# A gated cross-attention and ternary feed-forward block: new order of all five engines' lists, with the loads of x tiles 2 and 3 and of context 1 behind the gate weights

## The reference, cut to what matters

```python
# attention over the row's own layer norm: scores (512 x 512) are multiplied by it
qp = ctx @ Wq.T + bq ; kp = ctx @ Wk.T + bk
scores = (qp @ kp.T) * H**-0.5 * layernorm(x)
x = x + tanh(g_xattn) * softmax(where(mask, -inf, scores))
# feed-forward, activations quantised to 8 bits by row, weights to -1, 0, 1
def qlinear(x, w):
    ws = mean(abs(w)) + EPS ; wq = clip(round(w / ws), -1, 1)
    xs = max(abs(x), -1) / 127 + EPS ; xq = clip(round(x / xs), -128, 127)
    return (xq @ wq.T) * xs * ws
h = silu(qlinear(layernorm(x), w_gate)) * qlinear(layernorm(x), w_up)   # 2048 wide
x = x + tanh(g_ffn) * qlinear(h, w_down)
```

## Time and profile before

| what | value |
|---|---|
| median of 3 runs | 224.48 us |
| fastest, slowest run | 224.33, 224.86 us |
| span of the profiled execution, first to last instruction | 222.5 us |
| the profiled execution's own time | not given apart from its span |
| mean granted TensorE clock | 0.944 of full |
| PE, DVE, ACT, POOL busy | 199.3, 180.2, 124.5, 97.8 us |

### The profile page before, as it was taken

One profiled execution on the slowest core, in us unless ns is written; L12 is line 12 of the kernel. 1 busy time (PEld: TensorE's weight loads), 2 busy tenths in 40 slices (PEclk: granted clock), 3 DMA queues, 4 the chain that ended last, 5 costly groups with the idle time before them and its releaser, 6 DMA issues.

```text
span 222.5 us, 2846 instructions
## 1 busy us (share of the span) xinstructions
PE 199.3 (90%) x854; PEld 90.3 (41%) x854; DVE 180.2 (81%) x359; ACT 124.5 (56%) x165; POOL 97.8 (44%) x154
## 2 busy tenths in 40 slices
PE   8764008999999998999999999999999999999994
PEld 7221004344444344444444444444444444444441
...
GB/s 215 420 423 423 417 391 424 281 325 8 3 47 47 115 186 172 98 0 3 47 64 121 153 91 15 69 80 74 141 3 175 201 89 13 96 79 16 97 188 94
DMA packets 47360, 32.84 MB, mean 148 GB/s; under 512 B 40944, under 2 KB 41072, under 8 KB 45808
## 3 DMA queue, kind: packets, MB, share of 16 engines
...
q10 hardware_dynamic: 144, 0.13, 0.3%
...
## 4 chain that ended last, share of the span: by engine, by line
PE 71%; DMA 14%; ACT 5%; DVE 4%; issue 2%; SPq 2%; DVEq 0%
PE pU L947 23%; PE pG L934 23%; PE pD L965 20%; DMA stage_b<-in_L_ffn_w_up 8%; DMA stage_a<-in_L_ffn_w_down 4%; PE pA L909 3%; ACT down_w L689 2%; DMA stage_b<-stage_b 2%; ACT L736 1%; ACT hid L736 1%; DVE abs_part L1345 1%; SPq L351 1%; PE pA L898 1%; ACT stage_b L743 1%; DVE am L1320 1%
## 5 line engine op out<-in xcount | busy, mean ns | idle before, releaser
L736 ACT ACTIVATE hid<-pG,act_g 128x512 f32<-128x512 f32 x64 | 43.6, 688 | 54.6 <-PE pG L934 54.4
L934 PE MATMUL pG<-gate_w,xqT 128*128 128x512 f16 x256 | 64.7, 388 | 1.4 <-DVE xqT L1303 0.8
L947 PE MATMUL pU<-up_w,xqT 128*128 128x512 f16 x256 | 62.7, 379 | 0.0
L965 PE MATMUL pD<-down_w,stage_b 128*128 128x512 f16 x256 | 57.3, 379 | 0.6 <-DMA stage_b<-stage_b 0.6
L1311 DVE TENSOR_TENSOR hid<-pU,hid 128x512 f32<-128x512 f32 x64 | 43.6, 685 | 11.1 <-PE pU L947 9.2
L934 PEld LDWEIGHTS pG<-gate_w,xqT 128*128 128x128 f16 x256 | 25.1, 100 | 37.0 <-issue 8.0
L965 PEld LDWEIGHTS pD<-down_w,stage_b 128*128 128x128 f16 x256 | 24.9, 98 | 31.8 <-issue 2.3
L947 PEld LDWEIGHTS pU<-up_w,xqT 128*128 128x128 f16 x256 | 25.1, 98 | 31.3 <-issue 1.7
L743 ACT ACTIVATE stage_b<-hid,inv 128x1024 f16<-128x1024 f32 x15 | 16.9, 1139 | 7.8 <-DVE inv L1329 7.8
L560 POOL TENSOR_SCALAR out_scale<-den,act_e,down_k 128x1 f32<-128x1 f32 x16 | 5.9, 371 | 33.4 <-DVE den L1326 33.4
L909 PE MATMUL pA<-kT,qT 128*128 128x512 f32 x26 | 15.4, 678 | 4.9 <-ACT kT L709 4.9
...
## 6 DMA issues: line engine op xcount, KB each, us to landing
stage_a<-in_L_ffn_w_gate SPq DMA_DIRECT2D x4, 1024.0 KB, 11.2
stage_b<-in_L_ffn_w_up SPq DMA_DIRECT2D x4, 1024.0 KB, 19.2
stage_a<-in_L_ffn_w_down SPq DMA_DIRECT2D x4, 1024.0 KB, 9.0
stage_b<-in_x SPq DMA_DIRECT2D x2, 1024.0 KB, 5.3
...
```

The source lines that it names most:

```text
L736: act.activation(hid[:, t % NH, n * 512:(n + 1) * 512], pG[c % NG][:, :], ACT.Silu, scale=act_g[:, t:t + 1]).then_inc(silu_done, 1)
L934: ins = pe.matmul(pG[c % NG][:, :], xqT[:, t // TILES % 2, t % TILES, k, :], gate_w[:, n, k, :], start=k == 0, stop=k == KD - 1)
L947: ins = pe.matmul(pU[c % NU][:, :], xqT[:, t // TILES % 2, t % TILES, k, :], up_w[:, n, k, :], start=k == 0, stop=k == KD - 1)
L965: ins = pe.matmul(pD[t % ND][:, :], hidT[:, t % 2, k, :], down_w[:, k // KD, k % KD, :], start=k == 0, stop=k == KI - 1)
```

## The change

It renews the order of all five lists, and beside this:

- `chunk`: tiles 2 and 3 are interleaved by group as tiles 0 and 1 are.
- The q projection of batch 1 goes to `pG[1]`, k of batches 0 and 1 to `pG[0]`; score(3) goes to `pA`, not to `pD[1]`. Projections no longer wait for one another's copy but for the last user of their bank (`wait_pA`). The first two gate groups wait for k and q of batch 1 to be copied out of `pG`.
- `ABS_BY` becomes `ABS_PIECES`: all abs sums on ACT (gate's chunk 3 in two halves), but for one half chunk of up on DVE.
- `SIGN_BY`: gate's chunk 0 and down's chunk 2 are rounded by DVE (V), gate's others by POOL.
- POOL's rounds don't wait for the bound of the chunk before. The negative of a group's maximum is replaced by the negative of `rstd1`, computed in `rstd`. `rgate` is computed for a group at once.
- SP loads x tiles 2 and 3 and context 1 behind the four gate chunks, x tiles 4-7 before the up chunks, and down's chunks 1 to 3 behind transposes. Stores stand later.

```diff
 def chunk(t, n):
-    return 2 * n + t if t < 2 else NC * t + n
+    return 2 * NC * (t // 2) + 2 * n + t % 2 if t < TILES else NC * t + n
...
-        first_banks = [pA, *pU, pD[-1]][:TILES]
+        q_banks = [pA, pG[1], pA, pA]
+        k_banks = [pG[0], pG[0], pA, pA]
+        score_banks = [*pU, pA]
...
-        RESIDUAL_BY = "VPVVPPPPPPPVPPPP"
-        CENTRE_BY = "APAAAAAAAPVPVAVV"
-        QUANTISE_BY = "PPPPPPPPAAVAVPVV"
+        RESIDUAL_BY = 'VPPVPPPPPVPPPPVP'
+        CENTRE_BY = 'VPAAVAAAVPVAAPPV'
+        QUANTISE_BY = 'PPPPPPPAVPPAVPPA'
...
-        HQ_BY = ["PA", "AP", "AA", "AA", "PA", "PA", "AP", "AA",
-                 "PA", "PV", "PP", "AV", "PA", "AP", "VV", "PV"]
+        HQ_BY = ['PA', 'AP', 'VP', 'PA', 'PV', 'AA', 'AP', 'PA', 'PA', 'PV', 'PP', 'PV', 'VP', 'PA', 'VV', 'PA']
...
-        ABS_BY = ["AAAV", "AVAA", "AAAA"]
-        SIGN_BY = ["QXXX", "QQQX", "XXQQ"]
+        ABS_PIECES = [[(0, 0, 2048, 'A'), (1, 0, 2048, 'A'), (2, 0, 2048, 'A'), (3, 0, 1024, 'A'), (3, 1024, 2048, 'A')], [(0, 0, 2048, 'A'), (1, 0, 2048, 'A'), (2, 0, 2048, 'A'), (3, 0, 1024, 'V'), (3, 1024, 2048, 'A')], [(0, 0, 2048, 'A'), (1, 0, 2048, 'A'), (2, 0, 2048, 'A'), (3, 0, 2048, 'A')]]
+        SIGN_BY = ['VQQQ', 'QXQX', 'XQVQ']
...
             load_ctx(0)
-            sp.dma_start(masks_u8[:, :], masks).then_inc(mask_loaded, 16)
             load_x(0)
-            load_x(1)
-            load_ctx(1)
+            load_masks()
             load_w(0, 0)
             load_w(0, 1)
             load_w(0, 2)
             load_w(0, 3)
+            load_x(1)
+            load_ctx(1)
+            load_x(2)
             load_w(1, 0)
             load_w(1, 1)
             load_w(1, 2)
             load_w(1, 3)
+            load_ctx(3)
+            load_w(2, 0)
             load_ctx(2)
-            load_ctx(3)
-            load_x(2)
-            load_w(2, 0)
+            load_x(3)
+            transpose_x(4)
             load_w(2, 1)
+            transpose_x(5)
+            transpose_hidden(1, 1)
             load_w(2, 2)
             load_w(2, 3)
...
-                if m or n:
-
-                    wait_ternary(pool, *divmod(NC * m + n - 1, NC))
...
             def project_k(b):
-                pe.wait_ge(q_ready, b + 1)
-                pe.matmul(pA[:, :], wk_s[:, :], ctx_s[:, b % NQ, :], start=True, stop=True).then_inc(k_done, 1)
+                if b >= 2:
+                    wait_pA(pe, "k", b)
+                elif b == 1:
+                    pe.wait_ge(k_ready[0], 1)
+                pe.wait_ge(ctx_loaded[b], 16)
+                pe.matmul(k_banks[b][:, :], wk_s[:, :], ctx_s[:, b % NQ, :], start=True, stop=True).then_inc(k_done, 1)
...
+            def weight_round(m, n):
+                dve.wait_ge(winv_done, m + 1)
+                dve.tensor_scalar(chunk_of(m, n), stages[m][:, n, :], winv[:, m:m + 1], None, ALU.mult)\
+                   .then_inc(w_round_dve, 1)
```

More of the change, by code:

```diff
@@ L592, in _ @@
             quantise_x(0)
[L593 to L594 removed]
+            quantise_x(1)
+            rstd(1)
+            exp_bias(1)
+            weight_round(0, 1)
+            weight_round(0, 2)
+            valid_sums(1)
+            gate_scales(0)
+            residual1(2)
+            weight_round(0, 3)
+            std2(1)
+            weight_round(1, 0)
+            quantise_x(2)
+            quantise_x(3)
+            mask(2)
             up_scales(0)
[L596 removed]
@@ L1395, in _ @@
+            inverse_x(0)
+            stats1(3)
+            score(2)
+            score(3)
+            mask_and_max(2)
+            mask_and_max(3)
             weight_scale(0)
-            stats2(1)
-            weight_abs(1, 1)
+            weight_round(0, 0)
+            copy_xT(0)
             weight_bound(0, 0)
+            weight_bound(0, 1)
+            stats1(4)
+            stats1(5)
             gate_sums(1)
-            absmax_x(0)
-            weight_bound(0, 1)
-            absmax_x(1)
@@ new lines, in _ @@
+            stats2(8)
+            stats2(9)
+            centre(8)
+            product(6, 3)
+            absmax_x(8)
+            absmax_x(9)
+            inverse_std2(4)
+            inverse_x(4)
+            quantise_x(8)
+            product(7, 0)
+            absmax_hidden(5, 1)
+            inverse_hidden(5)
+            product(7, 1)
+            product(7, 2)
+            stats2(10)
+            centre(10)
+            product(7, 3)
+            product(8, 0)
+            residual2(3)
@@ L1503, in _ @@
+            absmax_hidden(6, 0)
+            stats2(11)
+            absmax_hidden(6, 1)
+            absmax_x(10)
+            absmax_x(11)
+            reciprocal_scale(4)
+            inverse_x(5)
+            inverse_std2(5)
+            residual2(4)
+            inverse_hidden(6)
             stats1(12)
-            product(4, 3)
-            mask_and_max(11)
-            product(5, 0)
-            absmax_hidden(4, 1)
             stats1(13)
-            inverse_hidden(4)
-            product(5, 1)
+            score(12)
@@ L1579, in _ @@
+            absmax_x(12)
+            stats2(13)
+            product(10, 3)
+            product(11, 0)
+            absmax_x(13)
+            inverse_x(6)
+            inverse_std2(6)
+            quantise_x(12)
+            residual1(14)
+            stats2(14)
+            inverse_hidden(9)
+            quantise_hidden(9, 1)
+            product(11, 1)
+            absmax_x(14)
+            product(11, 2)
             residual2(7)
-            quantise_hidden(9, 1)
-            product(10, 3)
+            product(11, 3)
```

1043 lines of the change are left out of this document (513 added, 530 removed).

## The result

The changed kernel takes 225.44 us (median of 13 runs, 224.08 to 226.65), the kernel before 224.33 in the same job (13 runs, 223.88 to 224.86): ratio 1.0052, 95% interval 1.0033 to 1.0070. Forecast was 218.8. It is slower by half a per cent, and its runs spread over 2.6 us against 1.0.

A forecast was written before the change was run, and what follows sets the result against it. TensorE's stream was taken as the bound: its start, work and losses. up(2,1) at 56.0 plus 155.3 for 180 units, losses of 1.3 and 1.1, and 5.15 after TensorE's end gave 218.8 us; forecast range 217 to 220.6, wider 215.0 to 224.0.

The forecast's parts named there:

- Loads, batch 0, first and third gate units: Head: gate chunk 0 lands at 9.6, context 1 at 19.0; first gate unit starts at 27.7, third at 33.3.
- weight_scale(1) gives 36.2: Head, DVE: the inverse scale of up comes at 36.2 us, no earlier than before.
- up(0,0) at 40.2, or 41.4: Head, TensorE: first up unit starts at 40.2 us, or 41.4 if two gate units run at half clock.
- up(2,1) ... I take 56.0: End of the head, TensorE: up(2,1) reached at 55.4 to 56.6 us, taken as 56.0, with 27 units done.
- the residual of 1.22: Head: residual1(0) on DVE took 1.22 beside POOL's mask add, 0.72 later; taken as a sign of DVE and POOL contending.
- The lists then run without a stall: Head, after up(1,1)'s wait at 48.5 to 49.7: no stall up to up(2,1) at 55.4 to 56.6.
- Losses of 2.4 after 56: TensorE after 56 us: 1.3 lost as before, and 1.1 more for a thinner cushion on DVE.
- Rival 2: Down's weights come late, behind transpose_hidden(1,1), if DVE is 22% slow over 29 us: 225.3, slower than before; chance 0.13.
- the cover of 0.4: Before weight_sum(2): abs of down's last chunk ends at 81.3, TensorE arrives at 81.7, leaving 0.4 us spare.
- Tail at nothing: End of kernel: reordered last gates and residual cost nothing; if the cover of 0.8 is gone, up to 1 us.
- POOL's rounds lose their wait ... POOL runs ahead: POOL: its weight rounds no longer wait for the bound in front (4.81 idle before one); counted at nothing.
- Rival 1: Head: TensorE's clock stays half to the first up, up(0,0) starts at 45.4, 4.6 later: 223.4; chance 0.12.

The follow-up runs named there:

- e13: e11 with DVE's eight clamps of gate and up weights replaced by statistics of the same time alone (clamping left out): 218.81 us, ratio 0.9741.
- e11: The changed kernel with down chunks 1 to 3 loaded ahead of transposes, pair 3's scales early, stores 4 to 11 issued as tiles are ready: 220.79 us.
- e5: The changed kernel with down chunks 1 to 3 loaded early, and inverse_std2(3) on DVE and gate_scales(3) on POOL moved earlier: 221.69 us, ratio 0.9892.
- e3: The changed kernel with stores 4 to 11 issued as their tiles are ready, not in one block at the end: 224.36 us, ratio 1.0003.
- e7: The changed kernel with gate's chunk 0 rounded by ACT, not DVE: 227.49 us, ratio 1.0141.
- e9: The changed kernel with its head reordered around the fifth and sixth scores and the inverse scale of up: 226.83 us, ratio 1.0112.
- e16: e11 with POOL's roundings of gate and up chunks again waiting for the clamp of the chunk in front: 224.90 us, ratio 1.0006.
- e15: e11 with DVE's half absolute sum of up chunk 3 given to ACT, nothing left out: 219.10 us, ratio 0.9772.

## Why the prediction was wrong

The forecast was 6.6 us too low: up(2,1) 3.2 late, 3.7 more lost behind it, 0.7 more from the last matmul to the end of the span (3.9 for 3.2), less 1.0, since the profiled execution was 1.0 slower than the median (the median stands 0.94 over its span and not 1.95).

- *Loads, batch 0, first and third gate units*: right. Chunk 0 landed at 9.4 (forecast 9.6), context 1 at 18.8 (19.0), the first unit came at 28.2 (27.7), the third at 33.55 (33.3). One table load came first and none before exp, as taken.
- *"weight_scale(1) gives 36.2"*, *"up(0,0) at 40.2, or 41.4"*, *"up(2,1) ... I take 56.0"*: this step failed. They came at 38.6, 43.8 and 59.2. I added DVE's list up with each shape's time alone; 3.6 us of exclusion were missing in a head in which DVE is busy 38.4 of 41 us. I had the mechanism in hand, with the residual of 1.22, and weighed it for the first rounding alone; that one took 1.28 and no more, and the clamps behind it paid. e13 gives back 2.1 of e11's 2.9. What e13 still lacks to 56.0 (0.9) goes with exclusion that its edit does not touch: the residual at 1.69 and POOL's pair at 5.01 for 3.94 stand before its score(6); no run took these away. The clock, which fell again at 38, made up(0,0) 1.6 later (6.2 us from score(6) to up(0,0), 4.6 in e11 at full clock), but at up(2,1) 0.25 of it is left at most: DVE begins its products at 51.29 in both kernels.
- *"The lists then run without a stall"* after up(0,0) held; but the four gate units behind score(6) waited for DVE, which the walk through the lists had not shown because it had DVE 2 us earlier.
- *Losses of 2.4 after 56*: 6.1. Rival 2 came about in part: transpose_hidden(1,1) stood at 73.6 and not 70.2, the weight sum at 86.6 and not 81.7. A late head alone would have moved both alike: the transpose came 3.4 late and TensorE reached the sum 3.1 late (84.8). What used up the cover of 0.4 was the way behind the transpose: 13.0 us from its start to the end of the last abs, where I had 11.1; the last chunk was there 11.0 after that start (84.55), not 9.1. I had priced the rival only by DVE's durations (22%). What I did not see at all is the second: gate_scales(3) behind POOL's down roundings (5.96 for the two, beside DVE's rounding of down's chunk 2: the same exclusion). e5 takes both away for 3.75.
- *Tail at nothing, "or up to 1"*: e3 gives 1.1, e11 0.9. In the profiled executions the block of stores costs from 0.7 (the changed kernel) to 2.1 (e7, e9) behind the last residual.
- *"POOL's rounds lose their wait ... POOL runs ahead"*, at nothing: the walk through the lists had POOL run ahead, which is worth some 4 (e16), but not the price, the clamps' exclusion, 2.0 (e13).
- *Rival 1*: the clock did not stay at half, but it fell back; in e7 it stayed and the time was 227.5.
- The sum's other terms were sound: in e11, with the stalls and the tail removed, TensorE ends 1.4 us over 180 units of 0.863 behind up(2,1) (2.4 taken), 3.2 before the end of the span, and the 220.8 is 2.0 over the forecast, with up(2,1) 2.9 late. That e15's 219.1 is 0.3 from the forecast is luck: it has another edit in it.
